# A causal mask folded into the row maxima: VectorE adds it and takes the maximum in one instruction per head and part, in place of two mask products on TensorE

## The reference, cut to what matters

```python
att = jnp.einsum('bhqd,bhkd->bhqk', q, k) * (1.0 / math.sqrt(HS))
causal = jnp.tril(jnp.ones((Tx, Tx), dtype=bool))
att = jnp.where(causal[None, None, :, :], att, -jnp.inf)
att = jax.nn.softmax(att, axis=-1)
y = jnp.einsum('bhqk,bhkd->bhqd', att, v)
```

## Time and profile before

| | |
|---|---|
| median of 3 runs | 2321.46 us (2321.45 to 2325.84) |
| the profiled execution: its own time | 2324.15 us |
| the profiled execution: its span | 2322.4 us |
| PE busy in the span | 2134.6 us (92%) |
| DVE busy in the span | 1578.2 us (68%) |
| ACT busy in the span | 1084.3 us (47%) |
| POOL busy in the span | 1577.8 us (68%) |
| the reductions of lines 841 and 844 | 161.8 us and 213.4 us busy, 384 of each |
| granted TensorE clock, mean | 0.968 |

### The profile page before, as it was taken

The page is one execution under the profiler, slowest core; times in us unless marked ns, Lnnn a source line. Parts: engine busy times, 40 slices in busy tenths (PEclk is TensorE's granted clock), DMA queues, the critical chain, the costliest instruction groups (busy, mean ns, idle before and its releaser), DMA issues. The chain is left out here.

```text
span 2322.4 us, 49007 instructions
## 1 busy us (share of the span) xinstructions
PE 2134.6 (92%) x14772; PEld 2068.0 (89%) x14772; DVE 1578.2 (68%) x4286; ACT 1084.3 (47%) x2850; POOL 1577.8 (68%) x2317
## 2 busy tenths in 40 slices
PE   5999999999999999999999479999999999999980
PEld 5999999999999999999988379999999999999980
DVE  5577777777777777777777446666666666665656
ACT  2444444444444444444444245454545445454545
POOL 3366767676767676767656657777777777777756
PEclk8999999999999999999999689999999999999995
DMA  7656565656565656565644143201010101001338
GB/s 204 144 132 146 132 145 130 145 129 145 129 145 130 142 130 142 128 144 128 144 97 99 32 107 56 42 5 29 4 31 5 30 5 29 4 4 24 56 44 334
DMA packets 235842, 223.54 MB, mean 96 GB/s; under 512 B 90647, under 2 KB 216066, under 8 KB 234688
## 3 DMA queue, kind: packets, MB, share of 16 engines
q1 hardware_dynamic: 135872, 147.40, 25.0%
q10 hardware_dynamic: 45568, 59.31, 11.2%
q0 software_dynamic: 54272, 15.20, 5.4%
HBM read 154.56 MB, written 98.38 MB: 109 GB/s over the span
## 5 line engine op out<-in xcount | busy, mean ns | idle before, releaser
L1159 POOL DMA_INDIRECT x_tokens<-yout,e_entry x240 | 383.6, 1598 | 182.5 <-DVE yout L1340 136.1
L668 PE MATMUL Y<-p,vp 128*102 128x198 f32 x1536 | 360.9, 344 | 14.8 <-ACT ysb L490 8.8
L1355 DVE TENSOR_TENSOR a<-UP,gate 128x384 f32<-128x384 f32 x320 | 178.5, 558 | 220.2 <-ACT gate L1295 214.7
L446 POOL DMA_INDIRECT expert_lists<-entry,slot x256 | 290.3, 1134 | 54.1 <-issue 54.1
L495 ACT ACTIVATE p<-ST 128x396 f32<-128x396 f32 x384 | 190.9, 497 | 261.3 <-PE ST L640 254.8
L1144 POOL DMA_INDIRECT rows<-x_wide,e_entry x240 | 249.5, 1040 | 78.8 <-issue 71.9
L1295 ACT ACTIVATE gate<-GT 128x384 f32<-128x384 f32 x320 | 157.8, 493 | 298.2 <-PE UP L1237 298.2
L141 POOL TENSOR_TENSOR word_p<-word_p 1x1 f32<-1x1 f32 x416 | 89.1, 214 | 294.0 <-ACT p L497 282.1
L412 POOL TENSOR_TENSOR x_lo<-x,x_hi 128x396 fp32r<-128x396 f32 x192 | 205.4, 1072 | 80.9 <-ACT x_hi L466 79.2
L668 PEld LDWEIGHTS Y<-p,vp 128*102 128x102 f32 x1536 | 221.7, 170 | 29.6 <-issue 8.8
L841 DVE TENSOR_REDUCE rm<-S 128x2 f32<-128x256 f32 x384 | 161.8, 421 | 106.5 <-PE S L659 104.0
(11 more groups left out here) (212 smaller groups left out, 6640.8 us busy)
## 6 DMA issues: line engine op xcount, KB each, us to landing
x<-in_xt ACTq DMA_DIRECT2D x180, 198.0 KB
q<-qk_features SPq DMA_DIRECT2D x384, 74.2 KB
k<-qk_features SPq DMA_DIRECT2D x192, 148.5 KB
qk_features<-qk_hi SPq DMA_DIRECT2D x96, 198.0 KB, 2.8
qk_features<-qk_lo SPq DMA_DIRECT2D x96, 198.0 KB, 3.8
rb<-rd ACTq DMA_DIRECT2D x128, 74.2 KB
t_x<-x_tokens SPq DMA_DIRECT2D x15, 576.0 KB, 8.2
out<-t_o ACTq DMA_DIRECT2D x15, 576.0 KB, 8.2
```

The lines of the kernel that those rows point to most:

```text
L446: pool.indirect_dma_start(d["lists"][:, :], bass.IndirectOffsetOnAxis(ap=slot[o][0:REAL[t], t, c:c + 1], axis=0), entry[o][0:REAL[t], t, c ...
L668: return pe.matmul(Y[0:VW1, 0:TI], v0, p32[b][:, hh, 0:TI], start=start, stop=stop)
L1159: pool.indirect_dma_start(d["x1"][:, :], row_of(cc, t), yout[q][:], None, bounds_check=N - 1, oob_is_err=False, compute_op=ALU.add)\
L1355: dve.tensor_tensor(a32[m % 2][:], UP[m % 2][:, 0:TILE3], gate[m % 2][:], ALU.mult)\
```

## The change

The two mask products and the two bf16 tables that they read are gone; the last matmul of scores_second signals s_s. On VectorE the two reductions become a Words.wait and four tensor_tensor_reduce, one for each head and part. Each adds a table of 0 and -1e30 (later, float32 in SBUF) to the scores in PSUM, writes the sums as bf16 into a buffer that nobody reads (masked), and folds them with max into one column of rm. The old reductions wrote the negated maximum; now the sign is turned in the copy to nm, which carries scale=-1.0.

```diff
@@ attention_block, buffers and loads
-        masks = sb("masks", [P, 4, P], BF16)
-        identb, maskb, onesb, lowb = (masks[:, n, :] for n in range(4))
+        masks = sb("masks", [P, 2, P], BF16)
+        later, masked = sb("later", [P, P + TI], F32), sb("masked", [P, 4, TI], BF16)
+        onesb, lowb = (masks[:, n, :] for n in range(2))
...
@@ ScalarE
-                            act.activation(nm[im][0:NH, :], src[0:NH, 0:TI], ACT.Copy)\
+                            act.activation(nm[im][0:NH, :], src[0:NH, 0:TI], ACT.Copy, scale=-1.0)\
...
@@ TensorE
                 pe.matmul(S[0][:, b * P:(b + 1) * P], qt[rows, im, b, j, 0:P],
-                          kt[rows, im, j, 0:P], start=(b == 0), stop=False)
+                          kt[rows, im, j, 0:P], start=(b == 0), stop=(b == 1))
...
-            def mask_scores():
-
-                own = S[1][0:T1, 0:TP].rearrange("p (h c) -> p h c", h=2)[:, :, P:TI]
-                pe.matmul(own, identb[0:T1, 0:T1], repeat(maskb[0:T1, 0:T1], 2), start=False, stop=True)
-                pe.matmul(S[0][:, 0:2 * P], identb, repeat(maskb, 2), start=False, stop=True).then_inc(s_s, 1)
...
-                        scores_second(im, j, 1, qs, ks)
-                        mask_scores()
+                        scores_second(im, j, 1, qs, ks).then_inc(s_s, 1)
...
@@ VectorE
-                        dve.wait_ge(s_s, n + 1)
-                        dve.tensor_reduce(rm[im][:, 0, j:j + 7:6],
-                                          S[0][:, 0:2 * P].rearrange("p (h c) -> p h c", h=2),
-                                          AX.X, ALU.max, negate=True)
-                        dve.tensor_reduce(rm[im][0:T1, 1, j:j + 7:6],
-                                          S[1][0:T1, 0:TP].rearrange("p (h c) -> p h c", h=2),
-                                          AX.X, ALU.max, negate=True).then_inc(s_m, 1)
+                        words.wait((s_s, n + 1), (s_m, n))
+                        for b in range(2):
+                            col = b * (NH // 2) + j
+                            dve.tensor_tensor_reduce(
+                                out=masked[:, b, 0:P], in0=S[0][:, b * P:(b + 1) * P], in1=later[:, 0:P],
+                                scale=1.0, scalar=LOW, op0=ALU.add, op1=ALU.max,
+                                accum_out=rm[im][:, 0, col:col + 1])
+                        for b in range(2):
+                            col = b * (NH // 2) + j
+                            ins = dve.tensor_tensor_reduce(
+                                out=masked[0:T1, 2 + b, :], in0=S[1][0:T1, b * TI:(b + 1) * TI],
+                                in1=later[0:T1, P:P + TI], scale=1.0, scalar=LOW, op0=ALU.add, op1=ALU.max,
+                                accum_out=rm[im][0:T1, 1, col:col + 1])
+                        ins.then_inc(s_m, 1)
```

More of the change, by code:

```diff
@@ L58 @@
 FAR = 1.0e6
+LOW = -3.0e38
 FAR_ROW = 1000000
@@ L296, in attention_block @@
         loads = [(wpt, "wpt"), (wg, "wg"), (bpc, "bpc"), (bv, "bv"), (bp, "bp"), (postab, "pos"), (biastab, "bias")]
-        late_loads = [(bqk, "bqk"), (ident, "ident"), (masks, "masks"), (iota8, "iota8"), (kbase, "kbase"),
+        late_loads = [(bqk, "bqk"), (ident, "ident"), (masks, "masks"), (later, "later"), (iota8, "iota8"), (kbase, "kbase"),
                       (valid, "valid"), (tid, "tid")]
@@ L646, in scores_first @@
                 pe.matmul(S[0][:, b * P:(b + 1) * P], qt[rows, im, b, j, 0:P],
-                          kt[rows, im, j, 0:P], start=(b == 0), stop=False)
+                          kt[rows, im, j, 0:P], start=(b == 0), stop=(b == 1))
             def scores_second(im, j, b, qt, kt):
                 rows = slice(0, ROWS_QK)
-                pe.matmul(S[1][0:T1, b * TI:(b + 1) * TI], qt[rows, im, b, j, P:TI],
-                          kt[rows, im, j, :], start=(b == 0), stop=False)
-            def mask_scores():
-                own = S[1][0:T1, 0:TP].rearrange("p (h c) -> p h c", h=2)[:, :, P:TI]
-                pe.matmul(own, identb[0:T1, 0:T1], repeat(maskb[0:T1, 0:T1], 2), start=False, stop=True)
-                pe.matmul(S[0][:, 0:2 * P], identb, repeat(maskb, 2), start=False, stop=True).then_inc(s_s, 1)
+                return pe.matmul(S[1][0:T1, b * TI:(b + 1) * TI], qt[rows, im, b, j, P:TI],
+                                 kt[rows, im, j, :], start=(b == 0), stop=(b == 1))
             def values(im, j, b):
@@ L1524 @@
     ins["ident"] = np.eye(P, dtype=f32)
-    ins["masks"] = np.stack([np.eye(P), np.where(n[None] > n[:, None], -1e30, 0.0), np.ones((P, P)),
-                             n[:, None] < n[None]], axis=1).astype(bf16)
+    ins["masks"] = np.stack([np.ones((P, P)), n[:, None] < n[None]], axis=1).astype(bf16)
+    ahead = np.where(n[None] > n[:, None], np.float32(-1e30), np.float32(0.0))
+    ins["later"] = np.concatenate([ahead, np.zeros((P, P), f32), ahead[:, 0:T1]], axis=1)
     ins["iota8"] = np.broadcast_to(np.arange(E, dtype=f32), (P, E))
```

## The result

The changed kernel takes 2387.7 us (2383.87 to 2391.63, 4 runs), the one before 2323.14 us on the same chip: 64.6 us more, a ratio of 1.0277 (95% interval 1.0255 to 1.0299). Forecast were 2367 us and a range of 2298 to 2465. The sign, the size and the place of the loss came out. Of the prices behind them that of the mask did too; those of the word and of the writing-out did not, and the clock's fall had been given a chance of 0.01.

The account below looks back on a forecast made before the run. TensorE was taken to set the pace, with VectorE late in some stretches. Three stretches summed to a 40.40 us body, 1.58 more; over 30 bodies + 47 us gave 2371, or 2367 us against the median, range 2298 to 2465.

Parts of the forecast that it names:

- What bounds the kernel: TensorE sets the pace, busy 390.68 of 400 us; VectorE has a quarter of its time to spare, unevenly spread.
- the turn of steps 5 to 7: Step 5 to step 7 of a body, on VectorE: 2.53 + 2R = 5.75 us against 4.35, 1.40 us lost.
- The mask's price: Two mask products fewer on TensorE save 0.18 us a step; steps 2 and 8 save nothing, waiting for ScalarE's copy.
- The four writing-out instructions: VectorE instructions writing out the running maximum: 0.115 us each, 0.46 us for four; almost hidden as a rival, chance 0.25.
- R: Time a step's maxima take on VectorE, to the start of what follows: 0.82 us before, 1.61 us after.
- the prediction's own formula: A body takes 27.52 + 8R us; it turns from loss to gain at R = 1.41 us.
- The word: VectorE instruction in front of a step's maxima, carrying the wait: 0.18 us, taken from rows of 0.20 and 0.14.
- The clock: Rival: TensorE's clock falls as it idles more, being busy about 90%; chance 0.01, no price of its own.
- Step 7 to step 1: Stretch of a body where VectorE is the later: 11.35 + 6R = 21.01 us against 20.29, 0.72 us lost.
- Step 1 to step 5: Stretch of a body keeping TensorE's length less three masks: 13.64 us against 14.18, 0.54 us won.
- Sum: Three stretches make a body of 40.40 us, 1.58 more; 30 bodies counted, + 47 us.

Follow-up runs that it names:

- e7: Changed kernel with twelve idle products that nobody reads on TensorE, between step 7's turned scores and its wait for the maxima: 2363.99 us, ratio 1.0177.
- e1: Changed kernel with the word before the maxima made a memset of one number, which reads nothing, same waits: 2324.18 us, ratio 1.0001.
- e2: Kernel before with only the word (words.wait, two SBUF operands) added before the two reductions, masks kept: 2389.52 us, ratio 1.0288.
- e5: Changed kernel with the word reading one SBUF operand (a tensor_scalar) instead of two: 2323.27 us, ratio 1.0001.
- e10: Kernel before with the same two waits before the reductions, but a memset without operands as the word: 2327.97 us, ratio 1.0005.
- e11: Changed kernel with the mask products kept on TensorE and the word reading one operand: 2391.65 us, ratio 1.0289.
- e9: Kernel before without mask products, its two reductions cut into four, with no table and no word: 2303.72 us, ratio 0.9901.

## Why the prediction was right or wrong

**What bounds the kernel, and the turn of steps 5 to 7: right in kind.** Scores and maxima take turns, the loss sits in step 6, and TensorE's busy share would have hidden it. Measured from step 5 to step 7: 6.33 us, forecast 5.75, before 4.35.

**The mask's price: right.** 0.18 us a step. That steps 2 and 8 wait for ScalarE's copy anyway was right for step 2 (3.19 us in both kernels). Step 8 became shorter, probably since ScalarE catches up while step 7 is slow: in e7, whose step 7 is short again, step 8 is 2.80 us in place of 2.46.

**The four writing-out instructions: wrong, and this was the number that I said decides.** I put 0.115 us on each. They cost 0; the four pairs take 0.99 us, just the main instructions' 0.97, so these also stream at the full rate. R without a hold is 717.02 to 718.08 us in that body's step 8, 1.06 us, not 1.61. By the prediction's own formula the kernel would then have been faster. So the sign was right while the step that carried it was not.

**The word: wrong in its price and in kind.** I took 0.18 us from two rows with 0.20 and 0.14. Unheld it is 0.07 to 0.08 (711.67 to 711.74 behind the maxima in the changed kernel). The 0.20 at 716.65 was a held word already. It ends at 716.92, and GpSimd's timeline of before has the subtraction up to 716.91:

```profile
715.89 1.02 POOL L412 TENSOR_TENSOR x_lo<-x,x_hi 128x396 fp32r<-128x396 f32 x1
```

The 0.14 at 717.24 was held too, behind the select of 717.01 (up to 717.41). A duration that differs between equal instructions was the sign to follow. What the word really costs is the rest of what GpSimd is doing, up to 1.19 us, in front of the maxima for which TensorE waits. e1, e2, e5 and e10 show it: 64 to 66 us by the word's second SBUF operand, where the second wait, one more instruction and a first operand cost nothing that shows. In the changed kernel this sum has the falls of the clock in it that the wait brings.

**The clock: wrong.** I gave its fall a chance of 0.01, and no price, because 35.35 busy us of 40 had kept 1.00. A mean over 40 us says nothing of one gap. TensorE's busy share was 92%, and it still fell to 0.50 in step 7 in 22 of 28 bodies, behind waits of 1.4 to 2.34 us. The wait in front of step 7 goes with it, but doesn't settle it alone: five bodies with waits of 2.24 to 2.33 us kept 1.00, and in e11 it fell behind 12 of 13 waits of 1.8 to 1.9 us. e7 prices it at 24 us net of its own overrun, 1.2 us of step 7. Part of the 64 us that the word costs in the changed kernel is this; in e2, with waits of 1.5 us at most, the clock fell in step 7 in only two of the bodies 1 to 28, and the loss in steps 5 and 6 was 1.96 us of a body by itself.

**Step 7 to step 1: size by accident.** Forecast 21.01 us, VectorE's sum. Measured 20.31: VectorE was not the later one there, its maxima being short, and the slow clock filled the gap; in e7, with the clock up, the same stretch is 3.53 + 2.80 + 4.23 + 3.46 + 3.41 + 2.02 = 19.45 us, TensorE's 19.39 of the prediction. **Step 1 to step 5:** forecast 13.64, measured 13.95; step 1 gave nothing.

**Sum.** Body 40.40 forecast, 40.6 measured in the window; from the whole time, 64.6 / 30 = 2.15 us a body against 1.58. Too high by the writing-out (4 × 0.115 × 8 = 3.7 us of a body), too low by holds and clock. That two wrong terms of opposite sign met near the measured body is luck. Of the 59.7 us between the spans of the two profiled executions, 53.2 stand in bodies 1 to 28 (1.90 us each) and 4.3 in body 0. The prediction's own addition, 2371 less 2.7, gives 2368 rather than 2367, which changes nothing.

What stays open: why the pairs of e1 cost some 20 us more than the four reductions of e9. Most of it stands in the first and last bodies and goes with falls of the clock; whether the pairs bring those about by the time that the memset and they take in front of the product or by reading a table was not told apart. Of the 30 us that e11 has above the sum of its parts, 10 are left beside the clock. Open too is when the preparation of an indirect DMA holds VectorE and when it doesn't, and why equal waits of TensorE were followed by a fall of the clock in one body and by none in the next.

## What to carry to other kernels

Before an instruction goes in front of something that another engine waits for, count its SBUF operands: with two, on VectorE beside a busy GpSimd, its price can be the rest of what GpSimd is doing (here always for a subtraction, at times for an indirect DMA), however small it is. An instruction that only carries a wait should read nothing, or one operand. And when a wait on TensorE grows to some 2 us in each turn of a loop, look at the granted clock microsecond by microsecond behind it, in more than one turn, and not at the mean; here idle work in the gap paid for itself. Last, ask whether the work moved is needed at all: with this data, the masks in front of the maxima were not.

## What the hardware showed that I had not expected

- An instruction that writes out VectorE's running maximum starts with the next main instruction (710.39 and 710.39) and costs nothing.
- Two GpSimd instructions back to back hold VectorE's word through both (713.29 to 714.20), so that cutting one in halves bought nothing.
- A matmul-free stretch of 2.33 us was followed by a granted clock of 0.50, and not at once: it was still 1.00 from 711 to 713 us and fell when TensorE was busy again. 22 of 28 bodies of the changed kernel had such a fall, and six had none.
- GpSimd's preparation of an indirect DMA holds such VectorE instructions too (e2 at 622.96), but only some: 27 of 88 words in e2, 1 of 56 in the changed kernel.
